# Two transformer layers on one core: layer-0 router weights computed at the end of the layer-1 experts, and written out when the attention begins

## The chip, the cores and the metric

The kernel runs on 1 core of one Trainium2 chip. The core has a matrix engine (PE, whose weight loads are shown as PEld), VectorE (DVE), ScalarE (ACT), GpSimd (POOL) and SyncE (SP), which in this kernel only issues DMA transfers. Each engine takes its own instructions in order; semaphores tie them together. The metric is device microseconds of one execution, and lower is better. The median of three timed runs is what a change is measured by.

## What is computed

Two layers over 16 sequences of 256 tokens of 128 numbers. Each layer adds an attention and a mixture of experts to its input. Layer 0 has a windowed softmax attention of 8 heads and an expert block with a router over 8 experts, of which two count:

```python
def _L0_ffn_ref(hidden, router_w, router_b, sw1, sb1, sw2, sb2, rw1, rb1, rw2, rb2):
    router_logits = flat @ router_w + router_b
    router_probs = jax.nn.softmax(router_logits, axis=-1)
    topk_probs, topk_idx = jax.lax.top_k(router_probs, TOP_K)
    weights = jnp.zeros_like(router_probs).at[jnp.arange(T)[:, None], topk_idx].add(topk_probs)
    ...
    h1 = jax.nn.gelu(jnp.einsum('td,edh->teh', flat, rw1) + rb1[None], approximate=False)
    expert_out = jnp.einsum('teh,ehd->ted', h1, rw2) + rb2[None]
    mixed = jnp.einsum('ted,te->td', expert_out, weights)
    return (shared_out + mixed).reshape(b, s, d)
...
xn = _layernorm(x, axis=-1)
x = x + _L0_attn_ref(xn, ...) + _L0_ffn_ref(xn, ...)
xn = _layernorm(x, axis=-1)
x = x + _L1_attn_ref(xn, ...) + _L1_ffn_ref(xn, ...)
```

The "router weights" of the title are `weights` above: eight numbers for each token, six of them zero. Layer 1 has 32 small experts and another router, whose weights follow their own path.

## The kernel before

**Tiling.** A step is two sequences, 512 tokens; there are eight steps, s = 0 to 7. The order of work is written out by hand, one program for each engine, in functions of the same names: `attention(s)`, `experts0(s)` and `experts1(s)` (step 1 has `experts0_and_chain1(s)` in place of `experts0`). In step s the engines do the layer-0 attention and experts of step s and then the layer-1 experts of step s - 1. So the loop body is attention(s), experts0(s), experts1(s), and next comes attention(s + 1). `experts1(s)` has already the first scores, maxima and exponentials of attention(s + 1) in its last part. An attention runs over eight units u (four pairs of heads, two sequences). For each unit PE makes scores (L530), DVE takes maxima (`maxima`, L1358), ACT exponentiates (`exps`, L1008), PE transposes (`turn`, L543), DVE copies the result out (`pt_copy`, L1369) and PE multiplies with the values (`weigh`, L555).

**Layer-0 router weights.** The logits of step n are made in experts1(n - 1), and `route0_top` and `route0_less` follow there. In unit 1 of attention(n), ACT takes the exponential (`exp0`, L1026, pr<-lg) and DVE makes the weights out of it (`route0_weights`, L1417 to L1421: four small instructions, the last one writes wr). When that is done (semaphore WEIGHTS0), SP writes wr, a number of 4 bytes at a time, to HBM (`weights_layer0`, L374, scratch<-wr, 128 x 32 numbers), waits until it has landed, and loads it back four times, spread over all partitions (L387, wb<-scratch, four transfers of 512 KB). DVE uses wb as it weighs each expert's output (`weigh0`, L1438).

**Denominators.** The softmax denominators of the attention are turned by PE after its last unit, copied by ACT, and written to HBM by SP (`denominators`, L409, scratch<-pt, 16 KB). SP waits for the landing and loads them back spread out (L422, wide<-scratch, two transfers of 512 KB). POOL multiplies them into the attention output in four parts (`normalise`, L1817, atc<-atc,wide). PE's product with the attention's output matrix (`attention_out`, L622, eight matmuls) waits for the fourth part. On POOL the order of experts0 in steps 2 to 6 is: `rope_turn` 0 (L1809, L1811, for the attention of the next step), normalise 0, rope_turn 1, `add0` 1 (L1823), normalise 1, rope_turn 2, add0 2, normalise 2, rope_turn 3, add0 3, normalise 3, then the rest of the add0s. `rope_turn` p waits for a shuffle on DVE (L1336, qks<-ps), which in turn waits for PE's projection p.

**SP's order.** All the transfers named here are issued on SP's queue, in program order: in step s the router weights of layer 0 out and in, the denominators out and in, the layer-1 weights out and in (L393, L404), the next input (L448), and the output of step s - 1 (`output`, L426, out<-wide). The last of these waits for `out_rows` (DVE, L1466), which in steps 2 to 7 is in unit 0 of the next attention. The wait for WEIGHTS0 is behind it.

Of the kernel before, what the change touches and what calls it, by code (L numbers as in the profile page):

```python
# [20 lines left out]
LAST = STEPS - 1  # L21
# [65 lines left out]
def two_layers(nc, A, out):  # L87
    pe, act, dve, pool, sp = nc.tensor, nc.scalar, nc.vector, nc.gpsimd, nc.sync
    with ExitStack() as ctx:
# [260 lines left out]
        def sp_program():  # L350
# [7 lines left out]
            def stage(n):  # L358
                if n >= 2:
                    w.wait_ge(*LOW.at(0, SPLIT_STAGED + n - 2))  # L360
                half, src, _ = staging(n)
                sp.dma_start(half, src).then_inc(STAGED[n % 2], 16)

            def weights_layer0(s):
                if s:
                    w.wait_ge(*WEIGHTS0.at(s))
                else:
                    w.wait_ge(*WT0.at(s))
                for k in range(RING):
                    w.wait_ge(*(wb_layer0(k, 0) if s == 1 else wb_layer1(RING + k, s - 2)) if s else (WB[k], 0))  # L370
                if s:
                    by_token = bass.AP(tensor=scratch0.tensor, offset=0, ap=[[1, P], [P, E0 * TILES]])
                    with nc.allow_non_contiguous_dma(reason="a weight of 4 bytes goes to each row"):
                        sp.dma_start(by_token, wr0[:, :, :].rearrange("p e t -> p (e t)")).then_inc(*SCRATCH0.one)  # L374
                else:
                    sp.dma_start(scratch0, wt0[:, :]).then_inc(*SCRATCH0.one)
                w.wait_ge(*SCRATCH0.at(s))
                if s == 0:
                    w.wait_ge(*LOW.at(0, SPLIT_W1 + 2))
                for k in range(RING):  # L380
                    if s == 1:
                        w.wait_ge(*WEIGHTED0.at(0, 2 * k + 1))
                    elif s:
                        w.wait_ge(*HH_WEIGHED.at(s - 2, 1 + 2 * (RING + k) + 1))
                    src = bass.AP(tensor=scratch0.tensor, offset=2 * k * TOK,
                                  ap=[[0, P], [TOK, 2], [1, TOK]])
                    sp.dma_start(wb[:, 2 * k:2 * k + 2, :], src).then_inc(WB[k], 16)  # L387
# [36 lines left out]
            def output(s):  # L424
                w.wait_ge(*OUT_ROWS.at(s))
                sp.dma_start(out[s], orow[:, :, :]).then_inc(*OUT.one)  # L426

            for s in range(STEPS):
                if s == 0:
                    stage(0)  # L430
                    stage(1)
                    stage(2)
                    stage(3)
                    stage(4)
                if s == 1:
                    stage(7)
                    stage(8)
                weights_layer0(s)
                if s == 0:
                    stage(5)  # L440
                    stage(6)
                denominators(s)
                if s:
                    for n in range(RING):
                        weights_layer1(s - 1, n)
                if s + 2 < STEPS:
                    w.wait_ge(*X1.at(s))
                    sp.dma_start(xin[:, s % 2, :, :], A["x"][s + 2]).then_inc(*X[s % 2].one)  # L448
                if s:
                    for n in range(RING, 2 * RING):  # L450
                        weights_layer1(s - 1, n)
                    output(s - 1)
            for n in range(2 * RING):
                weights_layer1(LAST, n)
            output(LAST)
# [498 lines left out]
        def act_program():  # L954
# [163 lines left out]
            def attention(s):  # L1118
                first, second = s == 0, s == 1
# [3 lines left out]
                for u in range(1, UNITS):  # L1123
                    exps(s, u, 0)
                    if u > 2 or u == 2 and s < 2:
                        out_cols(s, u - 2)
                    if u == 1 and not first:
                        exp0(s)
                    if u == 4 and first:
                        exp0(s)  # L1130
                    if u == 6 and first:
                        wt0_copy(s, score_bank(5, 1))
                    if u == 5 and second:
                        z1_cols(0, score_bank(4, 1))
                    exps(s, u, 1)
                    if u == 2 and s > 1:
                        out_cols(s, 0)
                    if u == 3 and second:
                        z1_rows(0)
# [70 lines left out]
            def experts1(s):  # L1210
                x, n, more = s - 1, s + 1, s < LAST
# [33 lines left out]
                if more:  # L1245
                    y1_high(s)
                    exps(n, 0, 0)
                    exps(n, 0, 1)
                lay1(x)

# [21 lines left out]
        def dve_program():  # L1272
# [303 lines left out]
            def attention(s):  # L1576
                first, second = s == 0, s == 1
# [6 lines left out]
                for u in range(UNITS):  # L1584
# [9 lines left out]
                        variance1(0)  # L1594
                    if u == 2 and second:
                        shifts(1, 0)
                    if u == 1 and not first:
                        route0_weights(s)
                    if u == 1 and first:
                        route0_top(s)  # L1600
# [95 lines left out]
            def experts1(s):  # L1696
                x, n, more = s - 1, s + 1, s < LAST
# [52 lines left out]
                y1_low(s)  # L1750
                if more:
                    maxima(n, 1)

            dve.wait_ge(*CONSTANTS.at(0))
            variance0(0)
# [349 lines left out]
```

## Time and profile before

| | us |
|---|---|
| Median of three timed runs | 1003.79 (1003.75 to 1005.33) |
| The profiled execution, its own time | 998.54 |
| Its span | 997.2 |
| PE busy | 960.6 (96%) |
| DVE busy | 671.9 (67%) |
| ACT busy | 508.5 (51%) |
| POOL busy | 434.2 (44%) |
| DMA, mean rate | 73 GB/s |

The profiled execution is 5.25 us shorter than the median of the timed ones; nothing in the profile says where those are spent. The clock granted to PE is at full speed in all 40 slices of the span. Times in the profile's rows are microseconds from the start of the span. In a timeline row the first number is the start and the second the length from first start to last end; "[0.99 <-POOL ...]" is how long the engine was idle before and what ended that. Rows with xN are N instructions merged. Buffer numbers are left out in names, so ps stands for all matrix-result banks, wr for wr0, pr for pr0, and lg for lg0.

### The profile page before, as it was taken

The numbers are of one execution on the slowest core, as the hardware profiler recorded it, in microseconds if no ns is written. First come the engines' busy times: TensorE is split into PE (matmuls) and PEld (weight loads), VectorE is DVE, ScalarE is ACT, GpSimd is POOL, SyncE is SP. The second block draws the span as 40 slices with busy tenths as digits, with TensorE's granted clock in tenths as the row PEclk, the third lists the DMA queues.
The fourth block names the chain that finished last, engine by engine and source line by source line (L and its number), as shares of the span: only waits on it lengthen the run. The fifth ranks groups of instructions, "written<-read, shape, count | busy, mean of one in ns | idle before, by whom it ended". The sixth has DMA issues, their size and how long they took to land.

```text
span 997.2 us, 13565 instructions
## 1 busy us (share of the span) xinstructions
PE 960.6 (96%) x4508; PEld 632.9 (63%) x4508; DVE 671.9 (67%) x1579; ACT 508.5 (51%) x1194; POOL 434.2 (44%) x343
## 2 busy tenths in 40 slices
PE   5899889999999999999999999999999999999988
PEld 3565566676666766677665766657666576657655
DVE  5857758686675876767766677757776476625923
ACT  3564674545745267362764537545475445635222
POOL 5856336651094501863037620565106541055343
PEclk9999999999999999999999999999999999999999
DMA  7050340610433114230252301522034310343071
GB/s 277 14 169 1 34 128 1 140 44 12 104 82 95 31 12 129 66 102 16 12 152 74 85 1 12 167 80 64 5 63 118 83 45 12 90 106 102 3 160 33
DMA packets 63237, 72.80 MB, mean 73 GB/s; under 512 B 33272, under 2 KB 34040, under 8 KB 62784
## 3 DMA queue, kind: packets, MB, share of 16 engines
q1 hardware_dynamic: 61744, 69.94, 28.1%
q10 hardware_dynamic: 1424, 2.00, 0.6%
q8 instruction: 36, 0.59, 0.3%
q14 instruction: 33, 0.27, 0.1%
HBM read 69.04 MB, written 2.88 MB: 72 GB/s over the span
## 4 chain that ended last, share of the span: by engine, by line
PE 75%; DVE 8%; POOL 6%; DMA 5%; issue 3%; ACT 2%; SPq 0%; DVEq 0%; ACTq 0%; POOLq 0%
PE ps L721 11%; PE ps L476 8%; PE ps L478 7%; PE ps L477 7%; PE ps L614 6%; PE ps L530 6%; PE ps L555 6%; PE ps L543 6%; PE ps L622 3%; DMA wide<-scratch 3%; PE ps L696 2%; DMA scratch<-pt 2%; POOL pt L1823 2%; POOL kr L1809 2%; POOL qr L1811 2%
## 5 line engine op out<-in xcount | busy, mean ns | idle before, releaser
L1116 ACT ACTIVATE wide<-ps 128x512 f32<-128x512 f32 x136 | 81.1, 596 | 214.4 <-PE ps L478 213.8
L1008 ACT ACTIVATE pw<-ps,nmax 128x256 f32<-128x256 f32 x256 | 119.0, 476 | 61.3 <-DVE nmax L1358 61.2
L1043 ACT ACTIVATE pw<-ps,w_cols 128x512 f32<-128x512 f32 x144 | 98.9, 689 | 99.7 <-PE ps L478 97.7
L1829 POOL TENSOR_TENSOR atc<-atc,wide 128x512 f32<-128x512 f32 x64 | 82.0, 1282 | 123.1 <-DVE atc L1567 123.1
L614 PE MATMUL ps<-pw,w_w 128*128 128x512 f32 x288 | 135.4, 592 | 0.0
L1809 POOL TENSOR_TENSOR kr<-qks,w_rope 128x512 f32<-128x512 f32 x32 | 43.7, 1366 | 167.6 <-DVE qks L1336 167.6
L1369 DVE COPY pt<-ps 128x512 f32<-128x512 f32 x128 | 83.2, 684 | 32.6 <-PE ps L543 32.4
L476 PE MATMUL ps<-yc,eg 128*128 128x512 f32 x128 | 94.3, 737 | 0.0
L1358 DVE TENSOR_REDUCE nmax<-ps 128x4 f32<-128x1024 f32 (+1 forms) x80 | 79.2, 1007 | 20.7 <-PE ps L530 20.7
L1829 POOL TENSOR_TENSOR pt<-pt,wide 128x512 f32<-128x512 f32 x48 | 61.7, 1284 | 64.1 <-DVE pt L1567 63.0
L476 PE MATMUL ps<-yc,w 128*128 128x512 f32 x144 | 80.0, 556 | 2.4 <-ACT pw L1043 2.4
L543 PE MATMUL ps<-ident,pw 128*128 128x128 f32 x512 | 75.8, 283 | 5.1 <-ACT pw L1008 3.2
L614 PEld LDWEIGHTS ps<-pw,w_w 128*128 128x128 f32 x288 | 53.5, 189 | 42.6 <-issue 37.7
L543 PEld LDWEIGHTS ps<-ident,pw 128*128 128x128 f32 x512 | 55.7, 141 | 37.2 <-issue 26.4
L555 PE MATMUL ps<-pt,vr 128*64 128x256 f32 x512 | 70.3, 395 | 4.1 <-DVE pt L1369 3.2
L1567 DVE TENSOR_TENSOR atc<-ps,wb 128x512 f32<-128x512 f32 x64 | 43.8, 686 | 44.9 <-PE ps L478 37.3
L530 PE MATMUL ps<-kr,qr 64*128 64x256 f32 x512 | 72.6, 402 | 1.1 <-DVE qr L1349 1.1
L1567 DVE TENSOR_TENSOR pt<-ps,wb 128x512 f32<-128x512 f32 x64 | 44.0, 688 | 41.1 <-PE ps L478 39.5
L721 PE MATMUL ps<-atc,w_ed 128*128 128x512 f32 x128 | 67.1, 606 | 0.4 <-POOL atc L1829 0.4
L721 PE MATMUL ps<-pt,w_ed 128*128 128x512 f32 x128 | 65.9, 599 | 0.0
L1817 POOL TENSOR_TENSOR atc<-atc,wide 128x512 f32<-128x512 f32 x32 | 43.7, 1365 | 42.7 <-DMA wide<-scratch 42.7
L477 PE MATMUL ps<-yc,w 128*128 128x512 f32 x144 | 56.8, 394 | 0.0
(224 smaller groups left out, 2137.3 us busy)
## 6 DMA issues: line engine op xcount, KB each, us to landing
wb<-scratch SPq DMA_DIRECT2D x128, 256.0 KB, 4.0
wb<-scratch SPq DMA_DIRECT2D x32, 512.0 KB, 6.3
wide<-scratch SPq DMA_DIRECT2D x16, 512.0 KB, 6.0
xin<-in_x SPq DMA_DIRECT2D x8, 256.0 KB, 2.7
out<-wide SPq DMA_DIRECT2D x8, 256.0 KB, 2.1
wb<-in_w SPq DMA_DIRECT2D x1, 1152.0 KB, 9.5
w_w<-in_w SPq DMA_DIRECT2D x1, 1152.0 KB, 12.6
w_ed<-in_ed SPq DMA_DIRECT2D x1, 1024.0 KB, 16.5
```

The source lines that it names most:

```text
L476: pe.matmul(bank(k), high, moving[:, 0, :], start=True, stop=False)
L477: pe.matmul(bank(k), high, moving[:, 1, :], start=False, stop=False)
L530: m = pe.matmul(ps[:, b, qt * SEQ:(qt + 1) * SEQ], qr[rows, p, q0:q0 + P], kr[rows, p, g * SEQ:(g + 1) * SEQ], start=False, stop=True, ski ...
L543: m = pe.transpose(bank(k)[:, j * P:(j + 1) * P], pw[:, u % 2, 2 * par + qt, kt * P:(kt + 1) * P], ident[:, :])
L555: m = pe.matmul(bank(b)[64 * par:64 * par + 64, 0:SEQ], vr[:, 2 * g + kt, 2 * p + par, :], pt[:, u % 2, 4 * par + 2 * kt:4 * par + 2 * kt ...
L614: pe.matmul(bank(k), w2[:, e, c, :], hid[:, n % 4, :], start=c == 0, stop=c == 1 and e < E0).then_inc(*DOWN0.one)
L721: pe.matmul(bank(ACC), sd[:, :] if c < 0 else ed[:, c, :], hh[(c + 1) % len(hh)], start=c < 0, stop=c == CH1 - 1).then_inc(*DOWN.one)
L1008: m = act.activation(pw[:, u % 2, j, :], ps[:, score_bank(u, par), qt * SEQ:(qt + 1) * SEQ], ACT.Exp, bias=nmax[:, u % 3, j:j + 1], scale= ...
L1043: act.activation(hid[:, n % 4, :], bank(UPS0[n % 2]), ACT.Gelu, bias=cols[:, C_B1 + 2 * e + c:C_B1 + 2 * e + c + 1], scale=1.0).then_inc(* ...
L1369: dve.tensor_copy(pt[:, u % 2, 4 * par:4 * par + 4, :].rearrange("p a q -> p (a q)"), bank(TURN_BANKS[par])).then_inc(*PT.one)
L1567: dve.tensor_tensor(hh[h], bank(k), wb[:, c % (2 * RING), :], ALU.mult).then_inc(*HH_WEIGHED.one)
L1829: pool.tensor_tensor(hh[h], hh[h], sgl[:, (c + 1) % 3, :], ALU.mult).then_inc(*HH_POOL.one)
```

## The change

`exp0` and `route0_weights` of steps 2 to 7 go from unit 1 of the attention to the end of the experts1 before it. SP's function is split: the write of wr (`weights_layer0_out`) stands ahead of the output of step s - 2, which before was at the end of step s - 1; the loads of wb follow. Steps 0 and 1 keep their order. No instruction is added or removed.

```diff
-            def weights_layer0(s):
+            def weights_layer0_out(s):
+
                 if s:
                     w.wait_ge(*WEIGHTS0.at(s))
                 else:
...
                 else:
                     sp.dma_start(scratch0, wt0[:, :]).then_inc(*SCRATCH0.one)
+
+            def weights_layer0(s):
                 w.wait_ge(*SCRATCH0.at(s))
...
+                weights_layer0_out(s)
+                if s > 1:
+                    output(s - 2)
                 weights_layer0(s)
...
                 if s:
                     for n in range(RING, 2 * RING):
                         weights_layer1(s - 1, n)
-                    output(s - 1)
+            output(LAST - 1)
             for n in range(2 * RING):
                 weights_layer1(LAST, n)
             output(LAST)
...
-                    if u == 1 and not first:
+                    if u == 1 and second:
                         exp0(s)
...
                 if more:
                     y1_high(s)
                     exps(n, 0, 0)
+                    exp0(n)
                     exps(n, 0, 1)
                 lay1(x)
...
-                    if u == 1 and not first:
+                    if u == 1 and second:
                         route0_weights(s)
...
                 if more:
                     maxima(n, 1)
+                    route0_weights(n)
```

On SP, from the end of one step's layer-1 weights (the last L404 row) to the denominators of the next step, before:

```order
L404 DMA wb<-scratch 64x2x512 x8
L426 DMA out<-wide 128x512
L374 DMA scratch<-wr 128x32x1
L387 DMA wb<-scratch 128x1024 x4
L409 DMA scratch<-pt 8x512
L422 DMA wide<-scratch 64x4x512 x2
```

and now:

```order
L407 DMA wb<-scratch 64x2x512 x8
L375 DMA scratch<-wr 128x32x1
L429 DMA out<-wide 128x512
L390 DMA wb<-scratch 128x1024 x4
L412 DMA scratch<-pt 8x512
L425 DMA wide<-scratch 64x4x512 x2
```

The write of wr is now ahead of the output, and the wait for the output rows stands between it and the loads of wb.

On DVE, from the maxima of unit 1 (the last experts1 row) into the next attention, the router weights before stand behind the reciprocal of unit 1:

```order
L1358 TENSOR_REDUCE nmax<-ps 128x4
L1369 COPY pt<-ps 128x512 x2
L1358 TENSOR_REDUCE nmax<-ps 128x2 x2
L1466 TENSOR_TENSOR wide<-x1s,ps 128x512
L1377 RECIPROCAL rden<-den 128x2x2
L1369 COPY pt<-ps 128x512 x2
L1358 TENSOR_REDUCE nmax<-ps 128x4
L1377 RECIPROCAL rden<-den 128x2x2
L1417 TENSOR_REDUCE sm0<-pr0 128x4
L1418 RECIPROCAL mx0<-sm0 128x4
L1419 TENSOR_TENSOR pr0<-pr0,mx0 128x32
L1421 SCALAR_TENSOR_TENSOR wr0<-mr0,pr0 128x4x8
```

and now ahead of the copies of unit 0:

```order
L1365 TENSOR_REDUCE nmax<-ps 128x4
L1424 TENSOR_REDUCE sm0<-pr0 128x4
L1425 RECIPROCAL mx0<-sm0 128x4
L1426 TENSOR_TENSOR pr0<-pr0,mx0 128x32
L1428 SCALAR_TENSOR_TENSOR wr0<-mr0,pr0 128x4x8
L1376 COPY pt<-ps 128x512 x2
L1365 TENSOR_REDUCE nmax<-ps 128x2 x2
L1473 TENSOR_TENSOR wide<-x1s,ps 128x512
```

The four instructions moved ahead by the copies, maxima and reciprocals of two units and by the output rows (L1466). They wait there for ACT's exponential.

On ACT, at the same place (the L1049 row is `lay1`, which closes experts1), before:

```order
L1008 ACT_TABLE_LOAD
L1008 ACTIVATE pw,den<-ps,nmax 128x256 x4
L1049 ACTIVATE pt<-ps,w_cols 128x512
L1008 ACTIVATE pw,den<-ps,nmax 128x256 x2
L1026 ACTIVATE pr0<-lg0 128x32
L1008 ACTIVATE pw,den<-ps,nmax 128x256 x6
```

and now:

```order
L1014 ACT_TABLE_LOAD
L1014 ACTIVATE pw,den<-ps,nmax 128x256 x2
L1032 ACTIVATE pr0<-lg0 128x32
L1014 ACTIVATE pw,den<-ps,nmax 128x256 x2
L1055 ACTIVATE pt<-ps,w_cols 128x512
L1014 ACTIVATE pw,den<-ps,nmax 128x256 x8
```

The small exponential (L1026, now L1032) stands ahead of two of unit 0's exponentials and of lay1. PE's and POOL's order is the same in both kernels.

## Rows read from the trace of the kernel before

**Rows 1.** The page, busy time, share of the span and instructions of PE

```profile
PE 960.6 (96%) x4508; PEld 632.9 (63%) x4508; DVE 671.9 (67%) x1579; ACT 508.5 (51%) x1194; POOL 434.2 (44%) x343
```

**Rows 2.** Waits of PE: total us, times, longest us

```profile
PE ps L622 <- POOL atc L1817: 3.1, 4, 1.3
```

**Rows 3.** Timeline of PE: attention_out of steps 2 and 5

```profile
296.95 3.70 PE L622 MATMUL ps<-atc,w_wo 128*128 128x512 f32 x8 [0.57 <-POOL atc L1817]
...
655.97 3.70 PE L622 MATMUL ps<-atc,w_wo 128*128 128x512 f32 x8 [0.99 <-POOL atc L1817]
```

**Rows 4.** Timeline of DVE: maxima of unit 1 for steps 2, 3, 4, 5, 7

```profile
236.99 1.22 DVE L1358 TENSOR_REDUCE nmax<-ps 128x4 f32<-128x1024 f32 x1 [0.92 <-PE ps L530]
...
356.94 1.23 DVE L1358 TENSOR_REDUCE nmax<-ps 128x4 f32<-128x1024 f32 x1 [0.92 <-PE ps L530]
...
476.02 1.23 DVE L1358 TENSOR_REDUCE nmax<-ps 128x4 f32<-128x1024 f32 x1 [0.92 <-PE ps L530]
...
595.62 1.23 DVE L1358 TENSOR_REDUCE nmax<-ps 128x4 f32<-128x1024 f32 x1 [0.92 <-PE ps L530]
...
836.56 1.23 DVE L1358 TENSOR_REDUCE nmax<-ps 128x4 f32<-128x1024 f32 x1 [0.92 <-PE ps L530]
```

**Rows 5.** Timeline of SP's queue in steps 1 and 5 (start, us to issue)

```profile
127.60 1.77 SPq L387 DMA_DIRECT2D wb<-scratch  x4
135.10 0.29 SPq L409 DMA_DIRECT2D scratch<-pt  x1
136.57 1.24 SPq L422 DMA_DIRECT2D wide<-scratch  x2
...
604.72 0.38 SPq L374 DMA_DIRECT2D scratch<-wr  x1
621.54 1.96 SPq L387 DMA_DIRECT2D wb<-scratch  x4
625.01 0.29 SPq L409 DMA_DIRECT2D scratch<-pt  x1
630.25 1.24 SPq L422 DMA_DIRECT2D wide<-scratch  x2
```

**Rows 6.** Waits of SP's queue: total us, times, longest us

```profile
SPq L387 <- DMA scratch<-wr: 109.6, 7, 16.4
```

**Rows 7.** Timeline of POOL: normalise 0 of steps 2, 4, 5, 6; normalise 3 of 5

```profile
278.92 1.28 POOL L1817 TENSOR_TENSOR atc<-atc,wide 128x512 f32<-128x512 f32 x1 [1.73 <-DMA wide<-scratch]
...
517.57 1.27 POOL L1817 TENSOR_TENSOR atc<-atc,wide 128x512 f32<-128x512 f32 x1 [1.37 <-DMA wide<-scratch]
...
634.51 1.28 POOL L1811 TENSOR_TENSOR qr<-qks,w_rope 128x512 f32<-128x512 f32 x1
637.92 1.29 POOL L1817 TENSOR_TENSOR atc<-atc,wide 128x512 f32<-128x512 f32 x1 [2.13 <-DMA wide<-scratch]
...
654.65 1.26 POOL L1817 TENSOR_TENSOR atc<-atc,wide 128x512 f32<-128x512 f32 x1
...
758.54 1.29 POOL L1817 TENSOR_TENSOR atc<-atc,wide 128x512 f32<-128x512 f32 x1 [2.42 <-DMA wide<-scratch]
```

**Rows 8.** Timeline of DVE: units 0 to 2 of step 5, and the shuffle for rope_turn 1

```profile
597.10 0.69 DVE L1369 COPY pt<-ps 128x512 f32<-128x512 f32 x1 [0.26 <-PE ps L543]
598.97 0.69 DVE L1369 COPY pt<-ps 128x512 f32<-128x512 f32 x1 [1.18 <-PE ps L543]
...
603.85 0.16 DVE L1417 TENSOR_REDUCE sm<-pr 128x4 f32<-128x32 f32 x1
...
604.58 1.28 DVE L1369 COPY pt<-ps 128x512 f32<-128x512 f32 x2
...
636.71 0.73 DVE L1336 STREAM_SHUFFLE qks<-ps 128x512 f32<-128x512 f32 x1
```

**Rows 9.** Timeline of ACT in step 5: lay1 and the router's exponential

```profile
596.66 0.69 ACT L1049 ACTIVATE pt<-ps,w_cols 128x512 f32<-128x512 f32 x1
...
598.15 0.23 ACT L1026 ACTIVATE pr<-lg 128x32 f32<-128x32 f32 x1
```

## The prediction, on record before the changed kernel ran

> **What bounds the kernel now.** I read the busy times first. PE is busy 96% of the span [rows 1], so a change that takes nothing from PE can gain only where PE stands still. The second view is therefore the waits of PE. Most are single events of the first steps. The one that repeats in the steady steps, and that has to do with this change, is attention_out (L622) waiting for POOL's last normalise: 3.1 us over four steps, the longest 1.3 [rows 2]. In steps 2 and 5 PE stood idle for 0.57 and 0.99 us there [rows 3].
>
> The third view checks this with a clock that needs no model of where a matmul ends: the time from one step to the next. The maxima of unit 1 stand at the same place of every step [rows 4]. Step 2 to 3 takes 356.94 - 236.99 = 119.95 us, 3 to 4 takes 119.08, 4 to 5 takes 119.60, and the two steps from 5 to 7 take 836.56 - 595.62 = 240.94. Step 3, in which L622 does not wait, is the shortest. The others exceed it by 0.87, 0.52 and 240.94 - 2 x 119.08 = 2.78, together 4.17 us. That is 1.1 more than the waits of [rows 2]: an idle time is counted only from the modelled end of the matmul before, and the first weight loads of L622 come late too.
>
> Why is POOL late? Follow step 5 backwards. Normalise 3 starts at 654.65 and ends at 655.91, and L622 starts at 655.97. Normalise 0 starts at 637.92 after an idle time of 2.13 us that the landing of wide ends [rows 7]; POOL has no other gap between. In the other waiting steps it is the same with 1.73, 1.37 and 2.42 us. The fourth view, SP's queue, says why wide lands late [rows 5]. SP writes the router weights at 604.72 and can load wb only at 621.54, 16.8 us later (seven such waits take 109.6 us, [rows 6]). The write of the denominators comes at 625.01, 3.5 us behind those 2 MB, and lands only at 630.25: 5.2 us for 16 KB. In step 1, where wb was issued 7.5 us ahead (127.60 against 135.10), the same write took 136.57 - 135.10 = 1.5 us. So the small write stands behind wb's bytes.
>
> **The change, part by part.**
>
> *The chain of wr starts earlier.* In step 5 the four DVE instructions start at 603.85 [rows 8] and wr is issued at 604.72, 0.87 later [rows 5]. Now they start when the maxima of unit 1 end, 595.62 + 1.23 = 596.85 [rows 4], so wr goes at about 597.7: 7.0 us earlier. With the same 16.8 us, wb is issued at 614.5, 10.5 us ahead of the denominators' write. That is more than step 1's 7.5, so I take step 1's 1.5 us for the write: wide is issued at 626.5 and not at 630.25, 3.75 us earlier. The bound from the other side is no gain here, 5.2 us as now. I take the first, because its distance is the nearer one.
>
> *What POOL makes of it.* Wide would land at 637.92 - 3.75 = 634.2, before POOL ends rope_turn 0 (634.51 + 1.28 = 635.8). The 2.13 us of idle time are gone, but rope_turn 1 needs the shuffle that starts at 636.71 and ends at 637.44 [rows 8], and normalise 0 is done at 637.05. So 0.4 us comes back there, and the chain to normalise 3 moves by 1.7 us. By the same subtraction from [rows 7] it moves by 1.3, 1.0, 1.7 and 2.0 us in steps 2, 4, 5 and 6. Needed are 0.87 and 0.52 in steps 2 and 4 and 2.78 in 5 and 6 together, against 3.7. The cover is there in each; PE then reaches L622 first, as in step 3. What is late next is PE itself: step 3 shows all that follows (add0, join, rows) keeping its distance.
>
> *Gain:* 4.2 us by the step clock; 3.1 us if only the idle times of [rows 2] came back. I take 4.2, since step 3 is a whole step that runs without the wait. Steps 0, 1 and 7 have no such wait and give nothing.
>
> *DVE's four instructions ahead of unit 0's copies.* They cost 604.58 - 603.85 = 0.73 us of DVE's time [rows 8]. The first copy started at 597.10 after an idle 0.26 us; now it starts at about 597.6 and ends at 598.3. DVE's next work cannot start before 598.97, since it waits for PE (idle 1.18). So 0.7 us of room is left, and PE needs that first copy only to use its bank again in unit 1. Cost on the path 0; without that cover up to 0.73 x 6 steps = 4.4 us. In unit 2 DVE is 0.73 us freer, but there it waits for PE anyway, so I count no gain.
>
> *ACT's exponential.* It is 0.23 us long [rows 9], and moves ahead of two of unit 0's exponentials and of lay1. They shift by up to 0.2, and unit 1's second half gets it back. From 0 to 0.2 x 6 = 1.2 us; I take 0, because lay1 at 596.66 feeds only PE's transposes that come after those of unit 0, 2 us later, and DVE's wait for this exponential ends before its maxima do.
>
> *SP.* Now wr is issued while SP otherwise waits for the output rows; the output (256 KB) goes behind it on the same queue, and the wait for wr's landing behind that. Behind SP's wait for WEIGHTS0 now stands the output of step s - 2, whose rows DVE makes after the weights, so it loses nothing. The wait for the output rows (made by DVE before 603.85 in step 5 [rows 8], 10 us before wr lands) holds nothing up. The denominators also wait for that output's landing, which has until 626. Cost 0.
>
> The sum against the profiled execution: 998.54 - 4.2 = 994.3, span 997.2 - 4.2 = 993.0. The median of the timed runs lies 5.25 above the profiled one for reasons that the trace does not show. I leave that distance as it is: 1003.79 - 4.2 = **999.6 us**, 0.42% faster. With the low end of the gain (3.1) and a further 0.9 of ACT's bound it is 1001.6; with all of 2.13 and the like won in a timed run that waits longer, 998.
>
> **The rivals.**
>
> *The insertion eats the gain.* If PE's start of the attention depends on the first copy or on ACT more than I read, up to (0.73 + 0.2) x 6 = 5.6 us come back: 1003.8 - 4.2 + 5.6 = 1005.2 in full, and 1001.8 to 1004.7 for parts. For it: both are put into the one place where four engines hand over. Against it: the 1.18 us of idle time and 0.7 us of room. The same "no difference" comes out if the timed runs do not have the L622 waits that the profiled one has; for that speaks the unexplained 5.25 us. Chance 16%.
>
> *Slower: the output behind wr delays wr.* The write of wr is 4,096 pieces of 4 bytes, and in the changed kernel 256 KB follow on the same queue while it is in flight. The point of decision: wr may take 16.8 + 7.0 = 23.8 us until wb goes no earlier than now. Beyond that each us delays the denominators, L622 and so each of steps 2 to 6 by a us: one us beyond is 1003.8 + 5 = 1008.8. Against it: the denominators' write shows that a small transfer waits for bytes ahead of it, and here the large one is behind; even an additional 5 us would stay inside the 7. The Trainium skill bears on this (DMA: Bandwidth & Descriptors, section Queues, rings and completion order): on each DMA engine descriptors are consumed in ring order, but data descriptors carry no barrier, so a later one may finish its write first. By the first half the output cannot push wr back; by the second it could share its last writes. No row of before has a transfer behind wr, so none shows which; it is why I give this case more than a token chance, 8%.
>
> *The change does not do what it says:* wr would be issued no earlier because DVE waits for ACT's exponential or SP is held. ACT's work ends before DVE's maxima (lay1, behind both, starts at 596.66 [rows 9]), so I put it into the 16% above.
>
> **How the numbers follow.** Forecast as worked out, 998.6 to 1001.6: 70%. More gain than that, because timed runs wait longer at L622: 6%, down to 997. No difference: 16%. Slower: 8%. A measurement of this kernel tells about 0.2% (2 us) from no change, so faster begins at 1001.8: 76%, same 16%, slower 8%. The range leaves out the slower case, half of the larger gain and the upper end of the no-difference case: 998.0 to 1003.8.
>
> **What the profile of the changed kernel would show.** Right: wr issued some 7 us earlier and wb about 10 us ahead of the denominators' write; that write landing in 1.5 us; no idle time of POOL before normalise 0, and instead 0.4 us before rope_turn 1; no wait of PE for L622; all steps near 119.1 us. Wrong: a landing of wr above 20 us, a wait of PE for pt or pw in units 0 and 1 that was not there, or step times that stay at 119.6 and more with L622 waiting for something else.

## The result: faster by more than forecast, and by less on another chip

| | median (lowest to highest), runs |
|---|---|
| kernel before, beside the changed kernel | 1003.24 us (1000.93 to 1005.33), 6 |
| changed kernel | 994.87 us (994.39 to 996.39), 6 |
| ratio | 0.9912, 95% interval 0.9886 to 0.9938 |

The forecast was 999.6 us, with a range of 998.0 to 1003.8. The change takes off 8.4 us and not 4.2, and the time lies 3.1 us below the range. The profiled execution of the changed kernel took 994.6 us with a span of 993.3 us. The prediction's sum for it was 994.3 and 993.0. So the profile was forecast to 0.3 us and the median was missed by 4.7.

Three views of the changed kernel. First the page: PE's busy line and the first line of the chain that ended last.

```profile
PE 957.6 (96%) x4508; PEld 632.2 (64%) x4508; DVE 670.7 (68%) x1579; ACT 508.6 (51%) x1194; POOL 434.4 (44%) x343
...
PE 87%; DVE 8%; issue 2%; ACT 2%; DMA 0%; POOL 0%; DVEq 0%; ACTq 0%; POOLq 0%
```

The same line of the chain in the kernel before:

```profile
PE 75%; DVE 8%; POOL 6%; DMA 5%; issue 3%; ACT 2%; SPq 0%; DVEq 0%; ACTq 0%; POOLq 0%
```

Against [rows 1] PE is busy 3.0 us less and DVE 1.2, the others differ by under 1 us. The chain has next to no DMA and POOL left in it (0%, after 5% and 6%). The waits of PE (total, times, longest) have no row for POOL's last normalise, which was [rows 2] before. The largest of those that repeat over the steps is now (3.2 us over eight times in the kernel before):

```profile
PE ps L561 <- DVE pt L1376: 4.6, 10, 0.9
```

(The line numbers of the changed kernel are higher by 1 to 8: attention_out is L628, the maxima L1365, pt_copy L1376, normalise L1825, SP's wr, wb, denominators and wide L375, L390, L412, L425.)

Next SP's queue in step 5, to be read beside [rows 5], and POOL and DVE of the same step beside [rows 7] and [rows 8]:

```profile
595.51 0.39 SPq L375 DMA_DIRECT2D scratch<-wr  x1
599.34 0.35 SPq L429 DMA_DIRECT2D out<-wide  x1
615.33 1.75 SPq L390 DMA_DIRECT2D wb<-scratch  x4
624.23 0.29 SPq L412 DMA_DIRECT2D scratch<-pt  x1
625.68 1.24 SPq L425 DMA_DIRECT2D wide<-scratch  x2
```

```profile
634.98 1.29 POOL L1825 TENSOR_TENSOR atc<-atc,wide 128x512 f32<-128x512 f32 x1
636.73 1.28 POOL L1817 TENSOR_TENSOR kr<-qks,w_rope 128x512 f32<-128x512 f32 x1 [0.46 <-DVE qks L1343]
```

```profile
593.48 1.22 DVE L1365 TENSOR_REDUCE nmax<-ps 128x4 f32<-128x1024 f32 x1 [0.92 <-PE ps L536]
594.62 0.17 DVE L1424 TENSOR_REDUCE sm<-pr 128x4 f32<-128x32 f32 x1
...
595.37 0.68 DVE L1376 COPY pt<-ps 128x512 f32<-128x512 f32 x1
596.83 0.69 DVE L1376 COPY pt<-ps 128x512 f32<-128x512 f32 x1 [0.77 <-PE ps L549]
```

Counted from the start of the maxima of unit 1, wr is issued at 2.03 us and not at 9.10. The denominators' write lands 1.45 us after its issue instead of 5.24, POOL's normalise 0 (the first of its two rows) starts without a gap, and there is 0.46 us before rope_turn 1.

Last the clock of the steps, as in [rows 4]. The maxima of unit 1 of steps 2 to 7 stand, in the form of the first of these rows, at 236.21, 355.29, 474.38, 593.48, 713.92 and 833.01. So the steps take 119.08, 119.09, 119.10, 120.44 and 119.09 us. One step is 1.36 us too long. That is no wait for POOL; it is looked at near the end.

### The profile page after: what moved, and what is told of

The parts are those of the page before. It is cut to its first block, busy times and chain, and to the rows that moved or that the text cites. A ratio compares the mean times of both kernels' runs of the same rounds, so it can differ in the third digit from the quotient of the medians.

```text
span 993.3 us, 13565 instructions
## 1 busy us (share of the span) xinstructions
PE 957.6 (96%) x4508; PEld 632.2 (64%) x4508; DVE 670.7 (68%) x1579; ACT 508.6 (51%) x1194; POOL 434.4 (44%) x343
## 4 chain that ended last, share of the span: by engine, by line
PE 87%; DVE 8%; issue 2%; ACT 2%; DMA 0%; POOL 0%; DVEq 0%; ACTq 0%; POOLq 0%
PE ps L620 12%; PE ps L727 11%; PE ps L482 9%; PE ps L484 9%; PE ps L483 9%; PE ps L561 6%; PE ps L549 6%; PE ps L536 6%; PE ps L628 3%; PE ps L702 2%; DVE pt L1376 1%; PE ps L477 1%; PE ps L517 1%; PE ps L507 1%; PE ps L691 1%
## 5 line engine op out<-in xcount | busy, mean ns | idle before, releaser
L1049 ACT ACTIVATE pw<-ps,w_cols 128x512 f32<-128x512 f32 x144 | 98.9, 689 | 100.3 <-PE ps L484 98.4
L1376 DVE COPY pt<-ps 128x512 f32<-128x512 f32 x128 | 83.8, 683 | 31.9 <-PE ps L549 31.5
L1365 DVE TENSOR_REDUCE nmax<-ps 128x4 f32<-128x1024 f32 (+1 forms) x80 | 79.2, 1006 | 20.6 <-PE ps L536 20.6
L1825 POOL TENSOR_TENSOR atc<-atc,wide 128x512 f32<-128x512 f32 x32 | 43.7, 1364 | 31.1 <-DMA wide<-scratch 31.1
```

The costliest lines, as they stand in the source:

```text
L1049: act.activation(hid[:, n % 4, :], bank(UPS0[n % 2]), ACT.Gelu, bias=cols[:, C_B1 + 2 * e + c:C_B1 + 2 * e + c + 1], scale=1.0).then_inc(* ...
L1376: dve.tensor_copy(pt[:, u % 2, 4 * par:4 * par + 4, :].rearrange("p a q -> p (a q)"), bank(TURN_BANKS[par])).then_inc(*PT.one)
```

## The experiments

The question is where the other 4.2 us come from. **Theory A (waits):** the timed executions of the kernel before wait longer at L622 than its profiled one, and the change takes all of that away. **Theory B (side effects):** the moved instructions or the new place of the output gain something of their own. **Theory C (the chip):** the profiled execution and the timed ones differ by something that no edit touches. Three chips were used, here called the first, second and third. All ratios are to runs of the kernel before on the same chip. The chip of the result above, and of the profile that the prediction was made from, is not on record. A chip was used in one stretch of time only, so what is called a difference between chips could be one between hours. The last column has the five times from one maxima of unit 1 to the next.

| kernel | chip | median us | ratio, 95% interval | steps 2 to 7 in its profile, us |
|---|---|---|---|---|
| before, reruns | first | 1003.23 | | |
| before_again | first | 1002.11 | 0.9994, 0.9978 to 1.0011 | 120.45 119.80 124.12 120.05 121.02 |
| before_rows | first | 994.87 | 0.9912, 0.9893 to 0.9931 | 119.10 119.07 119.09 119.10 119.08 |
| after_rows | first | 994.18 | 0.9915, 0.9895 to 0.9935 | 119.09 119.08 119.10 119.10 119.10 |
| sp_only | first | 1007.61 | 1.0040, 1.0019 to 1.0062 | 119.83 120.23 121.00 124.35 124.21 |
| before, reruns | second | 998.34 | | |
| compute_only | second | 994.95 | 0.9963, 0.9949 to 0.9977 | 119.09 119.08 119.09 119.08 119.08 |
| small_wb | second | 996.42 | 0.9978, 0.9967 to 0.9989 | 119.08 119.09 120.01 119.09 119.82 |
| dummy_pieces | second | 1000.48 | 1.0025, 1.0012 to 1.0039 | 120.89 119.88 119.68 120.44 119.70 |
| after_late | second | 1034.84 | 1.0362, 1.0342 to 1.0383 | 126.12 126.13 125.85 126.76 125.80 |
| before, reruns | third | 996.67 | | |
| after_again | third | 994.56 | 0.9968, 0.9955 to 0.9980 | 119.09 119.07 119.08 119.08 119.08 |
| compute_again | third | 994.17 | 0.9965, 0.9953 to 0.9977 | 119.07 119.09 119.08 119.08 119.09 |
| rows_again | third | 994.87 | 0.9979, 0.9967 to 0.9991 | 119.07 119.08 119.07 119.08 119.09 |

### The kernel before, profiled once more

No edit.

> The unchanged kernel before, for a second profile and more timed runs. Theory A (the L622 chain: wr's late landing keeps wb and then the denominators late, and by more in most runs than in the first profile): median 1000 to 1004 us, and the profile's steps 2 to 6 exceed 119.1 us each by what PE waits at L622; if this profile is 1003 us long, the waits at L622 sum to about 8 us instead of 3.1. Theory B (stalls of an engine whose 16 KB instruction fetch meets wr's 4,096 small writes): the length beyond 997 shows as waits at other places, mostly in units 2 to 6 of the attention, with L622 still near 3 us.

This execution took 1004.91 us, nearer the timed median of 1003.2 than the first profile, and so it is the profile that the prediction lacked. (Of the 33 executions of this kernel on the first chip the fastest took 998.58 us, on the other two chips 998.54 is an ordinary time. The first profile may be a rare fast execution, or one from another chip.) Waits of PE at L622, and SP's waits for wr's landing (total, times, longest):

```profile
PE ps L622 <- POOL atc L1817: 5.5, 4, 3.0
...
SPq L387 <- DMA scratch<-wr: 116.1, 7, 17.3
```

Against [rows 2] and [rows 6], 3.1 has become 5.5 and 109.6 has become 116.1. The five steps exceed 119.08 by 10.0 us together, where the first profile had 4.17 by [rows 4]. And 1004.9 - 10.0 = 994.9, as 998.54 - 4.17 = 994.4: both are within 0.5 us of the changed kernel's time. The expectation had asked for some 8 us of waits at L622, and the row shows 5.5. Three things make up the difference to 10.0. The weight loads of L622 come late too, as the prediction said. Step 4 has a stretch of low clock, shown below. And in steps 2 and 5 PE is already 1.1 and 0.5 us later than in an undisturbed step long before L622 (at 262.49 and 623.21 us), behind copies of DVE that start late; that is a stall of the kind that theory B of the expectation looked for, and no wait for POOL. Some 8.4 of the 10.0 us are left for L622 and the clock behind it. The worst step is step 4. Its SP, POOL and PE:

```profile
487.18 0.38 SPq L374 DMA_DIRECT2D scratch<-wr  x1
504.67 2.51 SPq L387 DMA_DIRECT2D wb<-scratch  x4
507.47 0.29 SPq L409 DMA_DIRECT2D scratch<-pt  x1
515.51 1.24 SPq L422 DMA_DIRECT2D wide<-scratch  x2
```

```profile
522.95 1.27 POOL L1817 TENSOR_TENSOR atc<-atc,wide 128x512 f32<-128x512 f32 x1 [4.68 <-DMA wide<-scratch]
```

```profile
540.51 5.40 PE L622 MATMUL ps<-atc,w_wo 128*128 128x512 f32 x8 [3.04 <-POOL atc L1817]
```

wr needs 17.5 us, so only 2.8 us lie between wb and the denominators' write, and that write takes 8.0 us. POOL idles for 4.68 us and PE for 3.04. Then there is something that no wait shows: the eight matmuls take 5.40 us and not the 3.70 of [rows 3]. Stretches of 2 us say why (columns: stretch, length, busy times of PE, PEld, DVE, ACT and POOL with their instructions, granted clock, DMA share, GB/s):

```profile
538.00:540.00 2.00, 0.00 (x0) 0.00 (x0) 1.37 (x3) 0.10 (x1) 2.00 (x2) 1.00 0.00 0
540.00:542.00 2.00, 1.49 (x3) 0.81 (x4) 0.27 (x2) 1.28 (x1) 1.86 (x3) 0.81 0.21 41
542.00:544.00 2.00, 2.00 (x3) 0.69 (x3) 0.56 (x1) 0.00 (x0) 1.86 (x2) 0.50 0.85 220
544.00:546.00 2.00, 2.00 (x5) 0.91 (x4) 0.06 (x1) 0.00 (x0) 0.50 (x1) 0.83 0.00 1
```

Behind the 3 us in which PE stood, the granted clock is 0.50 (1.2 instead of 2.4 GHz) for 3.4 us; it falls some 0.75 us after PE has begun again. Laid over an undisturbed step, PE is 3.2 us late where L622 starts and 5.0 late behind it: the low clock puts 1.8 us on top of the wait. The Trainium skill (TensorE: Matmul & The Clock Gate, Part 1: The HAM clock gate) says that the gate knows only these two levels, set by how busy PE was of late; this trace agrees, with 1.00 and 0.50 and mixed values only in stretches that hold an edge.

The same execution has a second such stretch at 138 us, outside the five steps, behind a wait of 2.36 us of PE for ACT; the first profile has one of 3.4 us from about 31 us on, which the page's tenths do not show. Low-clock stretches are not the main part of the gain, however. Of the runs of the kernel before whose mean granted clock is 1.000, the median is 1000.3 us on the first chip (one run; 999.7 for the two of before_again), 997.4 on the second (8 runs) and 996.1 on the third (5 runs). The changed kernel has 993.7 in such runs on the third (3 runs).

### The small pieces taken away, in both kernels

```diff
-by_token = bass.AP(tensor=scratch0.tensor, offset=0, ap=[[1, P], [P, E0 * TILES]])
+by_token = bass.AP(tensor=scratch0.tensor, offset=0, ap=[[E0 * TILES, P], [1, E0 * TILES]])
```

With this edit wb is loaded back in another order, so the kernel weighs with wrong numbers; it measures only the time of a write without small pieces.

> The kernel before, with wr written to HBM as 128 rows of 128 bytes and not as 4,096 pieces of 4 bytes (the layout that is loaded back is then another one, so the output differs). Nothing else moves. Theory A: wr lands in about 2 us and not 16, wb goes some 14 us earlier, no wait at L622, time 993 to 996 as the changed kernel. Theory B: as fast or faster, since the small writes are gone: 992 to 995. Rival C (the gain of the change comes from moving the DVE and ACT instructions): no gain, 1003.

> The changed kernel with wr written as 128 rows of 128 bytes (output differs, as above). Theory A: no more to gain, 994 to 995, within 1 us of the changed kernel, its step 5 of 120.4 us included. Theory B: the stall of 1.35 us in step 5 goes and all steps are 119.1; 992.5 to 993.5. Against the kernel before with rows, the difference is the price of the moved DVE and ACT instructions alone: I expect 0 +- 0.5 us.

before_rows has the order of the kernel before and issues wr just as late, but wr now lands in 1.4 us:

```profile
604.14 0.33 SPq L374 DMA_DIRECT2D scratch<-wr  x1
605.57 1.74 SPq L387 DMA_DIRECT2D wb<-scratch  x4
```

It has every one of its steps at 119.07 to 119.10 us, no wait at L622, and the median that the changed kernel has in the result, 994.87 us. So a time as good as the changed kernel's comes from landing wr sooner and moving nothing. That is for A and against B. With the rows, the old order and the new differ by 0.7 us of median within overlapping intervals: DVE's four instructions and ACT's exponential in their new place cost nothing that these runs can tell. The long step of the first profile of the changed kernel is gone in after_rows, as theory B expected, but its 994.18 us are above that theory's 992.5 to 993.5; after_again below lacks the long step too, with the pieces.

### SP's order alone, and the computation alone

sp_only is the changed kernel with `exp0` and `route0_weights` back in unit 1; the write of wr still stands ahead of the output. compute_only is the opposite: the weights are computed early, and SP's part is that of the kernel before.

> The changed kernel's order on SP (wr ahead of the output), with the exponential and the router weights computed in unit 1 as before. wr is issued within 0.3 us of where it was before, the output 3 us later. Theory A: as the kernel before, 1001 to 1004. If SP's order alone gave the gain, 995.

> The kernel before with the exponential and the router weights moved to the end of experts1 as in the changed kernel, but SP's order kept: the output of the step before stands ahead of wr. The output rows are ready at the same time as before, so wr is issued right behind the output, some 2.9 us earlier than before and not 7. wb is then 6 us ahead of the denominators' write. Theory A: most of the gain, L622 waits under 0.5 us in sum, no drop of PE's granted clock there: 994.5 to 997. Rival (SP's order carries the gain): 1001 to 1004.

sp_only is slower than the kernel before (1.0040), and slower than I expected. Step 5 of sp_only, then of compute_only:

```profile
606.17 0.39 SPq L375 DMA_DIRECT2D scratch<-wr  x1
606.60 2.11 SPq L429 DMA_DIRECT2D out<-wide  x1
625.13 1.74 SPq L390 DMA_DIRECT2D wb<-scratch  x4
```

```profile
599.52 0.36 SPq L426 DMA_DIRECT2D out<-wide  x1
600.06 0.38 SPq L374 DMA_DIRECT2D scratch<-wr  x1
616.60 1.78 SPq L387 DMA_DIRECT2D wb<-scratch  x4
623.06 0.29 SPq L409 DMA_DIRECT2D scratch<-pt  x1
625.13 1.24 SPq L422 DMA_DIRECT2D wide<-scratch  x2
```

With 256 KB issued right behind it, wr needs 17.5 to 19.8 us to wb in steps 2 to 7 of sp_only; in before_again, on the same chip, 16.5 to 17.8. On the third chip it is the same: 17.0 to 18.2 in after_again with the output behind wr, 15.3 to 16.8 in compute_again with the output ahead. In the mean over the six steps the output behind it makes wr 1.4 and 1.3 us slower. That is the mechanism of my slower rival. The output suffers more than wr: here, from its issue to its landing (shortest, median, longest), in sp_only and in the kernel before:

```profile
DMA to landing us min/median/max: 2.1/17.8/19.5
```

```profile
DMA to landing us min/median/max: 2.1/2.1/2.4
```

Issued 0.4 us behind the pieces, 256 KB take 17.8 us instead of 2.1, and their issue alone takes 2.11 us instead of 0.36. The profile shows no engine held up by that. On the old start of wr the later landing shows at once:

```profile
PE ps L628 <- POOL atc L1823: 8.8, 5, 3.0
```

Two of sp_only's L622 waits (2.8 us in step 5) are again followed by 3.4 us at half clock, and these are its steps of 124.35 and 124.21. In the changed kernel the 7 us of lead hide wr's delay. The Trainium skill (DMA: Bandwidth & Descriptors, section Queues, rings and completion order) says that descriptors are consumed in ring order but carry no barrier, so that a later one may finish its write first; that leaves room for what is seen, though no row says which part of the write is held up.

compute_only has the gain without SP's part: 994.95, and PE has no wait at L622. It issues wr only 2.7 us earlier than the kernel before, wb goes 5.7 to 7.5 us ahead of the denominators, and their write lands in 1.9 to 2.9 us. That is enough.

### The 2 MB of wb taken away

wb's loads of steps 1 to 7 fetch 16 numbers for each expert and partition, 64 KB a step; the rest of wb stays as it was, so the kernel weighs with wrong numbers. wr is as slow and as late as before.

```diff
-sp.dma_start(wb[:, 2 * k:2 * k + 2, :], src).then_inc(WB[k], 16)
+small = bass.AP(tensor=scratch0.tensor, offset=2 * k * TOK, ap=[[0, P], [TOK, 2], [1, 16]])
+sp.dma_start(wb[:, 2 * k:2 * k + 2, 0:16], small).then_inc(WB[k], 16)
```

> The kernel before, but the four loads of wb in steps 1 to 7 bring 16 numbers a row and not 512 (so most of wb keeps old values; the output differs). wr is as late as before. Theory A (the denominators' write is late only because it stands behind wb's 2 MB): it lands in 1.5 us, no wait at L622, 994 to 996. If the lateness came from wr's own small writes, it stays near 5 us and the time at 1001 to 1004.

```profile
603.37 0.38 SPq L374 DMA_DIRECT2D scratch<-wr  x1
620.70 1.91 SPq L389 DMA_DIRECT2D wb<-scratch  x4
623.66 0.29 SPq L413 DMA_DIRECT2D scratch<-pt  x1
625.13 1.24 SPq L426 DMA_DIRECT2D wide<-scratch  x2
```

The write of the denominators starts 3.0 us behind wb and lands in 1.47 us. With most of wb's bytes gone, the 3.9 to 8.0 us of the two profiles of the kernel before shrink to the 1.5 of step 1 of the first. So it is these bytes that hold it, and not the late hour or the 4-byte pieces. The wait at L622 is gone, and the median falls by 1.9 us on a chip on which the full gain is 3.4. So removing the wait in this way leaves 1.5 us of the gain out. Two steps of this profile are still 0.9 and 0.7 us too long; there DVE stalls in the middle of the attention, as below.

### A second write of 4,096 pieces, nobody waiting for it

This is before_rows (with its wrong weights), and right behind wr a write of 4,096 pieces of 4 bytes into a spare buffer:

```diff
+pieces = bass.AP(tensor=scratch3.tensor, offset=0, ap=[[1, P], [P, E0 * TILES]])
+w.wait_ge(*SCRATCH3.at(s - 2))
+sp.dma_start(pieces, tri_rows).then_inc(*SCRATCH3.one)
```

> The kernel before with wr written as 128 rows of 128 bytes (output differs), and right behind it, in steps 1 to 7, another write of 4,096 pieces of 4 bytes to a buffer that nobody reads. wr lands early, but the small writes are in flight as before, and wb goes behind them on the queue. Theory A: no wait at L622; 994 to 996, with a stall of about 1.3 us of PE behind DVE in a step now and then, as in step 5 of the changed kernel, if small writes that meet an instruction fetch make such stalls. Theory B (small writes themselves cost the time): 1001 to 1004.

1000.48 us lies between the two expected ranges, and neither was right. On this chip it is 0.25% slower than the kernel before. rows_again, the same kernel without the second write, has 994.87 us on the third chip.

```profile
606.98 0.33 SPq L377 DMA_DIRECT2D scratch<-wr  x1
607.35 0.43 SPq L380 DMA_DIRECT2D scratch<-w_tri  x1
608.41 11.74 SPq L393 DMA_DIRECT2D wb<-scratch  x4
628.63 0.28 SPq L415 DMA_DIRECT2D scratch<-pt  x1
631.32 1.24 SPq L428 DMA_DIRECT2D wide<-scratch  x2
```

wr lands in 1.4 us, but SP needs 11.7 us to issue wb's four loads behind the pieces (11.0 to 12.2 in steps 2 to 7; 1.7 to 4.1 in the other kernels), and though the last is issued 8 us ahead of the denominators, their write takes 2.7 us here and 2.2 to 4.9 in the other steps. The waits at L622 are small (0.8 us for two). Stalls of DVE in the middle of the attention, 1.57 us idle each, make up most of what steps 2 and 5 lose; here that of step 5:

```profile
619.13 0.69 DVE L1376 COPY pt<-ps 128x512 f32<-128x512 f32 x1 [1.57 <-remote]
```

I had not reckoned with the slow issue: pieces cost also when nobody waits for their landing.

### wr held back in the changed kernel

```diff
+if s > 1:
+    w.wait_ge(*EXPS.at(s, 2 * 4 + 1))
```

SP issues wr only after the exponentials of unit 4.

> The changed kernel, with SP holding wr in steps 2 to 7 until ACT has done the exponentials of unit 4, about 5 us later than the kernel before issues it. Theory A: the denominators' write and the load of wide shift by 4 to 5 us against the kernel before, and L622 by as much in steps 2 to 6; waits of over 3 us there are followed by a stretch of half clock, 1.8 us more each: 1003 + 5 x (4.5 + 1.2) = about 1032 us, 1022 to 1040. If lateness of wr does not set the time: 995 to 1004.

1034.84 us, within the range expected. Past the edge the price is in full, and more than I counted: 36.5 us above the kernel before on this chip, where I had added 28.5 to 1003. wr goes 14.2 us behind the start of the maxima of unit 1, 12 later than in the changed kernel and 5 later than before; wb is issued 1.8 us ahead of the denominators, whose write takes 6 to 7 us, PE waits 14.7 us at L622 (L630 here) in five steps, and from 291 us on the span has five low-clock stretches of 3.4 us.

```profile
PE ps L630 <- POOL atc L1827: 14.7, 5, 3.1
```

The stretches do not belong one to one to these waits. Two come with the waits at L630 in steps 3 and 4. The other three follow waits for DVE, the first of them this one; the waits at L630 of steps 2, 5 and 6 (2.81, 2.74 and 3.05 us) have none behind them, the last of them being the second row:

```profile
290.72 0.92 PE L519 MATMUL ps<-wv,zc 128*128 128x512 f32 x2 [1.84 <-DVE qr L1358]
...
807.80 3.70 PE L630 MATMUL ps<-atc,w_wo 128*128 128x512 f32 x8 [3.05 <-POOL atc L1827]
```

The waits for DVE's qr are new, 8.0 us over seven times at L519. POOL's rope_turn 1 stands behind its wait for wide in the order of work, which would delay what follows from it; I did not trace it further.

### The changed kernel and its half on a third chip

> The changed kernel as it is, beside the next two and the kernel before, all on one chip. So far the kernel before had a median of 1003.2 us on one chip and 998.3 us on another, while kernels in which TensorE no longer waits at the out tile's multiplications lay at 994 to 995 us on both. Theory A: what differs between chips is only how long the kernel before waits there, so this one gives 994 to 996 us here, whatever the kernel before gives (997 to 1005 us). Theory B: chips differ in something that all kernels feel, so the ratio to the kernel before is the same everywhere (0.991) and the time moves with it: 989.5 us beside 998.3, 994 us beside 1003.

> The changed order on VectorE and ScalarE with the old order of the transfers on SyncE, once more, now on the same chip as the changed kernel. The early computation alone moves the write by the 3.3 us and wb's landing with it; the new place of the write and of the output in SyncE's order should bring nothing further: within 0.15% of the changed kernel (994 to 996 us). If the output's new place behind the write costs the 1 to 2 us of landing that it cost in the kernel with the order of SyncE alone, and the changed kernel sits close enough to the edge to feel it, this one is faster than the changed kernel by 0.5 to 2 us. If the output's old place beside the denominators' tile matters instead, it is slower by as much.

> The kernel before with the router weights written as 128 rows of 128 bytes, not 4,096 pieces of 4 bytes (what wb holds is then in another order, and the weights are not those of the reference). It is the measure of the kernel without the small pieces: 994 to 995.5 us if theory A holds, on this chip as on the first; it should move with the kernel before (989.5 us beside 998.3) if theory B does. If it is faster than the changed kernel by more than 0.5 us on the same chip, the small pieces still cost the changed kernel that, beyond the wait at the out tile.

Here the kernel before has 996.67 us, and the changed one 994.56: 0.32% faster, not 0.88%. Theory A holds in the main: what varies is how much the kernel before loses. The chip (or the hour) matters to it and hardly to the kernels without the wait. The changed kernel is at 994.6 and 994.9 in its two sets of runs while the kernel before goes from 1003.2 to 996.7. That this is the wait alone is argued: the kernel before has no profile on the second or third chip. compute_again is at 994.17 and rows_again at 994.87; among the three the runs show no difference. None of the kernels beats the changed one by more than they can tell.

after_again has steps of 119.07 to 119.09 throughout, so the 120.44 of the first profile of the changed kernel is not part of every execution. It came from here (DVE, then PE, step 5 of the first profile):

```profile
612.91 0.69 DVE L1376 COPY pt<-ps 128x512 f32<-128x512 f32 x1
614.72 0.69 DVE L1376 COPY pt<-ps 128x512 f32<-128x512 f32 x1 [1.12 <-PE ps L549]
```

```profile
613.46 1.13 PE L536 MATMUL ps<-kr,qr 64*128 64x256 f32 x8
615.47 1.08 PE L561 MATMUL ps<-pt,vr 128*64 128x256 f32 x8 [0.87 <-DVE pt L1376]
```

The copy waits for PE's transpose by the record, but PE had gone on to the next scores at 613.46 and then waited for the copy: DVE starts about 1 us late with nothing visible to wait for. wr's pieces and the output are in flight. The same is seen in small_wb and dummy_pieces, in steps 2 and 5 of before_again and in step 5 of sp_only, in none of the profiles with rows alone, and not in compute_only, compute_again and after_again. Each time 4-byte pieces were in flight. What holds DVE is open. I did not try it.

## Why the prediction was right, and where it was wrong

- **The chain of wr starts earlier:** 7.0 us forecast, 9.10 - 2.03 = 7.07 measured. wb was to be issued 10.5 us ahead of the denominators; it was 8.9, and 8.6 to 10.4 in the steps 2 to 7 of the two profiles of the changed kernel. The difference is wr's own time, 3.0 us more in step 5, less 1.4 us by which the stall of DVE puts off the denominators: I took 16.8 us, and with the output behind it it is 17.0 to 19.8. It costs nothing, since 8.6 is still enough for the 1.5 us landing, which was forecast as 1.5 and is 1.45 to 1.47 in all steps. I had bounded it from step 1's 7.5 us; compute_only shows that 5.7 do.
- **What POOL makes of it:** right. No gap before normalise 0, 0.46 us before rope_turn 1 (0.4 forecast), no wait at L622.
- **DVE's four instructions and ACT's exponential at nothing:** right. The first copy begins 1.89 us behind the start of the maxima (597.6 - 595.62 = 2.0 forecast), there is 0.77 us of idle time left behind it, and before_rows and after_rows differ by less than these runs can tell.
- **The gain in the profiled execution:** 4.2 us forecast. 998.54 became 994.6, 3.9 us less. This agreement is partly luck: 2.8 us are in the five steps (4.17 less the 1.4 of the DVE stall), the rest lies at both ends, where the first profile of the kernel before had a low-clock stretch of 3.4 us (at about 31 us, though the text ahead of the prediction calls the clock full in all slices) and the changed one's had only the last microsecond of the span below full clock.
- **The slower rival:** its mechanism exists, 1 to 2 us, and stays inside the 7 us that I set as its point of decision. Without the 7 us it makes the kernel 0.4% slower.
- **The step that failed** is "I leave that distance as it is: 1003.79 - 4.2". I carried 5.25 us of unexplained time across the change as if it were none of its business. Most of it was the same wait. In the second profile of the kernel before the steps lose 10.0 us and not 4.17, some 8.4 of them at L622 and by the clock behind it, and what remains, 994.9, is close to the medians of the kernels here that have no wait at L622: 994.2 to 995.0, but for small_wb with 996.42. The term of the sum that was mis-sized is the gain: 4.2 us in the execution that I had before me, 8.4 in the timed ones beside it, 3.4 on the second chip (by compute_only) and 2.1 on the third. I had named this case ("timed runs wait longer at L622") but gave it 6% and only 2.6 us more. Its lower end was also summed too short: "all of 2.13 and the like" is 7.65 us by [rows 7], which is 996.1 and not 998. And in the rival of no difference I took the unexplained 5.25 us as a sign that the timed runs might have no wait at L622; the runs showed the opposite. The only row that bore on it, the spread between executions, was at hand: a wait that varies between steps from 0 to 1.3 us and hangs on a landing that varies from 15.6 to 16.8 us is the first candidate for time that varies between executions.
- **What is open:** what holds DVE in its stalls, and why the kernel before waits longer on one chip than on another. before_again, on the first chip, has wr at 16.5 to 17.8 us against 15.6 to 16.8 in the first profile, and in step 4 wb's bytes move slower in the stretch that counts. Stretches of the two, behind wb's issue (before_again, then the first profile):

```profile
509.00:511.00 2.00, 2.00 (x12) 1.61 (x11) 0.49 (x3) 1.80 (x5) 0.00 (x0) 1.00 0.72 252
```

```profile
505.00:509.00 4.00, 4.00 (x17) 2.64 (x17) 2.26 (x15) 3.69 (x8) 0.00 (x0) 1.00 0.99 373
```

252 GB/s (188 in the 2 us before) against 373 fits a longer wait for the denominators; that the chip is what makes it so is not shown, with one profile each and the first one's chip unknown.

## What to carry to other kernels

If the change removes the only wait whose length varies, forecast the time after from the floor, that is the profiled time less that wait (994.3 here, 994.87 measured), and not from the median less that wait: the distance of median and profile is probably made of the same wait. This is one case. The gain was 0.3% to 0.9% here, while the time after moved by 0.3 us. Where a small write gates the path, look at what is issued just ahead of it, and at the size of its pieces: a layout of 128 rows gave the same time as the whole reordering, though with weights in the wrong order; what it would cost to put them right was not measured. And half of the change was enough: compute_again, without the new order on SP, is as fast.

## What was not expected of the hardware

- A write of 4,096 pieces of 4 bytes takes 14 to 20 us to be seen as landed, and 1.4 us as 128 rows. 256 KB issued 0.4 us behind it land only at about the same time, after 17.8 us. Much of the write's time passes with the DMA engines at rest. In step 4 of before_again, where wb can go only at 504.67, the stretch ahead of that (the last two columns: DMA share, GB/s) reads

```profile
499.00:503.00 4.00, 3.76 (x30) 2.29 (x27) 2.48 (x6) 2.93 (x10) 0.00 (x0) 1.00 0.00 0
```

- A wait of 3.04 us at L622 cost 5 us in before_again, since the granted clock fell to half for 3.4 us behind it. The same fall came with two such waits in sp_only and two in after_late. Three waits of 2.74 to 3.05 us in after_late had no such fall behind them, and one of 1.84 us elsewhere had. At L622 no wait of up to 1.7 us had one. So the length of a wait alone does not tell.
- Behind 4-byte pieces in flight the issue of transfers was slow (11.7 us for four loads, 2.11 for the output), and stalls of 0.5 to 1.6 us of DVE that no semaphore explains were seen only while pieces were in flight.
